# The second feed-forward of a two-layer block: 24 of its 32 token tiles sorted by expert, 8 left dense

## The reference, cut to what matters

```
logits = tanh(x @ Wg1.T) @ Wg2.T                    # x: 4096 x 256, layer-normed
_, top_idx = top_k(logits, 2)
scores[token, top_idx] = softmax(top_logits)         # zero for the other six
up   = einsum('td,ehd->teh', xt, Wup) + bup          # e: 8, h: 128
h    = silu(up)
down = einsum('teh,eoh->teo', h, Wdown) + bdown
out  = einsum('te,teo->to', scores, down)
x    = x + tanh(g_ffn[1]) * out
```

## Time and profile before

| | |
|---|---|
| time, median of 3 runs | 1808.64 us (1806.33 to 1809.66) |
| profiled execution | 1795.94 us, span 1794.1 us |
| first attention, first feed-forward | to about 830 us |
| second attention, last residual | 1520.2 us |
| last block's residual, end of the last output | 1790.6 us, 1794.1 us |

### The profile page before, as it was taken

The page is one execution under the profiler, slowest core; times in us unless marked ns, Lnnn a source line. Parts: engine busy times, 40 slices in busy tenths (PEclk is TensorE's granted clock), DMA queues, the critical chain, the costliest instruction groups (busy, mean ns, idle before and its releaser), DMA issues.

```text
span 1794.1 us, 42480 instructions
## 1 busy us (share of the span) xinstructions
PE 1619.7 (90%) x14740; PEld 1361.1 (76%) x14740; DVE 1160.6 (65%) x3029; ACT 738.2 (41%) x1508; POOL 423.3 (24%) x464
## 2 busy tenths in 40 slices
PE   3899999978998899998799999999999997799998
PEld 2566666656776689997688888888888886578887
DVE  5888888886567655456466666666666654465655
ACT  2466666652322225554333333333333332344443
POOL 3555555522224210000222111221221111000000
PEclk8999999999999999999899999999999998799999
DMA  7566666642101015433200000000000000000000
GB/s 203 114 126 126 124 125 126 125 74 67 38 30 42 24 42 156 143 124 111 77 27 22 20 26 21 20 23 27 20 26 20 21 15 6 1 24 12 12 24 24
DMA packets 127357, 107.07 MB, mean 60 GB/s; under 512 B 10442, under 2 KB 120195, under 8 KB 127020
## 3 DMA queue, kind: packets, MB, share of 16 engines
q1 hardware_dynamic: 121068, 89.07, 21.2%
q0 software_dynamic: 6208, 16.95, 2.9%
HBM read 49.22 MB, written 56.77 MB: 59 GB/s over the span
## 4 chain that ended last, share of the span: by engine, by line
PE 53%; DVE 24%; issue 10%; ACT 6%; SPq 3%; DVEq 1%; DMA 1%; ACTq 1%
PE bank L544 10%; PE bank L546 9%; PE bank L545 9%; PE bank L1020 4%; PE bank L606 3%; PE bank L615 2%; PE bank L1048 2%; PE bank L629 2%; PE bank L570 2%; DVE rm_b L2281 2%; PE bank L646 2%; DVE rs_b L2289 2%; DVE probs_b L2284 1%; DVE oT_b_lo L2273 1%; PE bank L633 1%
## 5 line engine op out<-in xcount | busy, mean ns | idle before, releaser
L544 PE MATMUL bank<-xT_b_hi,m_hi 128*128 128x256 f32 x512 | 154.1, 301 | 23.9 <-ACT qT L1390 12.0
L1411 ACT ACTIVATE probs_b<-probs_b 128x512 f32<-128x512 f32 x64 | 40.4, 632 | 324.9 <-DVE probs_b L2284 324.9
L1584 POOL TENSOR_TENSOR probs_b<-probs_b,rs_b 128x512 f32<-128x512 f32 x64 | 66.8, 1043 | 454.0 <-DVE rs_b L2294 453.7
L544 PE MATMUL bank<-n_hi,oT_b_hi 128*128 128x256 f32 x512 | 149.7, 292 | 5.8 <-DVE x L2252 5.8
L545 PE MATMUL bank<-xT_b_hi,m_lo 128*128 128x256 f32 x512 | 145.8, 285 | 0.0
L546 PE MATMUL bank<-xT_b_lo,m_hi 128*128 128x256 f32 x512 | 145.7, 285 | 0.0
L545 PE MATMUL bank<-n_hi,oT_b_lo 128*128 128x256 f32 x512 | 145.1, 283 | 0.0
L546 PE MATMUL bank<-n_lo,oT_b_hi 128*128 128x256 f32 x512 | 145.0, 283 | 0.0
L1194 ACT ACTIVATE probs_a<-probs_a 128x512 f32<-128x512 f32 x128 | 80.4, 628 | 114.4 <-DVE probs_a L1723 114.0
L1020 PEld LDWEIGHTS bank<-ctxT_b,qT 128*128 128x128 f32 x1024 | 125.2, 193 | 2.7
L544 PEld LDWEIGHTS bank<-xT_b_hi,m_hi 128*128 128x128 f32 x512 | 98.9, 193 | 30.5 <-ACT qT L1390 15.0
(11 more groups left out here) (316 smaller groups left out, 4786.7 us busy)
## 6 DMA issues: line engine op xcount, KB each, us to landing
sorted_x<-zeros SPq DMA_DIRECT2D x16, 2112.0 KB, 14.7
xg<-sorted_x SPq DMA_DIRECT2D x71, 128.0 KB, 2.1
sorted_y<-ys SPq DMA_DIRECT2D x71, 128.0 KB, 2.0
w_raw<-in_w SPq DMA_DIRECT2D x16, 408.0 KB, 3.8
x<-in_x SPq DMA_DIRECT2D x4, 1024.0 KB, 7.1
cx_raw<-in_ctx SPq DMA_DIRECT2D x32, 128.0 KB, 2.6
out<-x SPq DMA_DIRECT2D x8, 512.0 KB, 2.9
ctxT_a<-in_ctxT SPq DMA_DIRECT2D x16, 128.0 KB, 2.2
```

The costliest lines, as they stand in the source:

```text
L544: pe.matmul(dst, lh, rh, start=start, stop=False, skip_group_check=True)
L1584: pool.tensor_tensor(probs_b[b], probs_b[b], rs_b[:, b, :].unsqueeze(2).broadcast_to([P, G1, S]), ALU.mult).then_inc(s["b_probs"], 1)
```

## The change

The first 24 token tiles take the routed form in the second feed-forward; the last 8 stay dense, in two blocks.

- Routing goes into attention rounds 2 to 13 (`NR = 12`), always for the two tiles of two rounds before: TensorE gets `turn_f`, `logits_f`, `back_f` and `place_f`, ScalarE `xh_f` and `tanh_f`, VectorE `xl_f`, `largest_f`, `counts_f`, `slots_f` and at the round's end `norm_f`, GpSimd four scatters (`scatter_f`). `setup_f` is in round 1, the table of tiles (`table_f`, `places_f`) in round 14. The loop body now holds two rounds.
- The weights' halves move out of the rounds: ScalarE makes eight pieces of 512 columns in round 15, where the copies of queries were, and GpSimd the eight low pieces after its last probabilities.
- NJ1 = 31 tiles of 256 sorted rows follow the attention: loads with three buffers and two tiles ahead, two Silus for each tile on ScalarE (one full, one rounded), the bias added on VectorE in `y_x2`, and the expert's up-weights copied to a fixed place by GpSimd (`stage`). SyncE loads `bd1`, all eight output biases for all partitions (1 MB), before the third tile.
- The preparation of the first dense block stands between these tiles.
- After the last store GpSimd gathers 24 x 2 times (`gather_f`, three buffers); VectorE adds (`add_f`) nine tiles within the first dense block and fifteen within the second.
- The separate pass for mean and deviation (`stats`, with a square root on ScalarE) is gone; a reciprocal root on VectorE takes its place.

```diff
@@ SyncE @@
+            def load_rows1(j):
+                if j >= NX1:
+                    sp.wait_ge(s["x_xT_psum"], NJ + j - NX1 + 1)
+                row = sp.value_load(row1[0:1, j:j + 1], min_val=0, max_val=ROWS - R1)
+                sp.dma_start(xg1[j % NX1], xs_dram[ds(row, R1), :].rearrange("(t p) d -> p t d", p=P)).then_inc(s[f"x{j % NX1}_loaded"], 16)
+            def store_rows1(j):
+                sp.wait_ge(s["x_y_ready"], NJ + j + 1)
+                sp.dma_start(ys_dram[j * R1:(j + 1) * R1, :].rearrange("(t p) d -> p t d", p=P), ys1[j % NY1]).then_inc(
+                    s[f"x_stored{j % NY1}"], 16)
...
             sp.wait_ge(s["b_resid"], START + NA * 2)
+            sp.dma_start(bd1.rearrange("p e n -> p (e n)"), a["bdown"][0:E, :].rearrange("e n -> (e n)").unsqueeze(0).broadcast_to([P, E * D])).then_inc(s["w1_loaded"], 16)
+            sp.wait_ge(s["c_added"], NT)
+            for j in range(NJ1 + 2):
+                if j + NX1 - 1 < NJ1:
+                    load_rows1(j + NX1 - 1)
+                if j >= 2:
+                    store_rows1(j - 2)
@@ TensorE, attention round @@
-                scores1(i, 0)
+                scores1(i, 0, route is not None or late or last)
+                if route is not None:
+                    turn_f(i, route)
                 rest(outputs1, 3)
...
                 ahead(turn_x1)
+                if route is not None:
+                    logits_f(i)
                 rest(project1, 1, 1)
+                if route is not None:
+                    back_f(i)
                 ahead(queries1, 0)
                 scores1(i, 3)
                 turn_probs1(i, 0, last)
-                ahead(queries1, 1)
+                ahead(queries1, 1, route)
...
                 turn_probs1(i, 2, last)
+                if route is not None:
+                    place_f(i)
@@ TensorE, sorted tiles @@
+            for j in range(NJ1 + 2):
+                if j + 1 < NJ1:
+                    turn_x2(j + 1)
+                if j < NJ1:
+                    up_x2(j)
+                expert_f(j + 1)
+                if j >= 2:
+                    down_x2(j - 2)
+                if j == 10:
+                    turn(0, 0, 0)
+                if j == 13:
+                    turn(0, 0, 1)
+                if j == 16:
+                    pe.wait_ge(s["rw_split"], 3)
+                    logits(0, 0)
+                if j == 18:
+                    logits_back(0, 0)
+                if j == 22:
+                    turn_weights(0, 0)
...
+            for i in range(BLOCKS1):
+                block_(i, i % 2, i + 1 < BLOCKS1)
@@ ScalarE @@
+            def silu_x2(j):
+                n = NJ + j
+                e = act.value_load(exi1[0:1, j:j + 1], min_val=0, max_val=E - 1)
+                act.wait_ge(s["x_gu_psum"], n + 1)
...
+                act.activation(hs1[j % 2], bank[2 + j % 2][:, 0:R1], ACT.Silu, bias=bup[:, ds(e, 1)]).then_inc(s["x_silu"], 1)
+                act.activation(hgh1[j % NH1], bank[2 + j % 2][:, 0:R1], ACT.Silu, bias=bup[:, ds(e, 1)]).then_inc(s["x_hh_ready"], 1)
@@ GpSimd @@
+            def stage(j):
+                e = pool.value_load(exi1[0:1, j:j + 1], min_val=0, max_val=E - 1)
+                if j >= 2:
+                    pool.wait_ge(s["x_gu_psum"], NJ + j - 1)
+                for n, w in enumerate((w1_hi, w1_lo)):
+                    m = pool.tensor_copy(up1[j % 2][:, n], ffn1_view(w)[0][:, :, ds(e * P, P)])
+                m.then_inc(s["w1_split"], 1)
...
+            def gather_f(tile):
+                n = tile % NG1
+                if tile >= NG1:
+                    pool.wait_ge(s["c_added"], NT + tile - NG1 + 1)
+                done = s[("y_gathered", "y_gathered1", "y_gathered2")[n]]
+                for c in range(TOP):
+                    pool.indirect_dma_start(out=yg_f[n][:, c, :], out_offset=None, in_=ys_dram,
+                                            in_offset=bass.IndirectOffsetOnAxis(ap=place_of[:, c, tile:tile + 1], axis=0)).then_inc(done, 16)
@@ VectorE, attention round @@
                 weigh(0)
+                if route is not None:
+                    xl_f(i)
                 centre(2)
                 weigh(1)
                 if not last:
                     xT_low1(i + 1)
+                if not first and route is None and more:
+                    setup_f()
+                if route is not None:
+                    largest_f(i)
+                    counts_f(i)
                 centre(3)
...
                 if not last:
                     mask_row(i + 1)
+                if route is not None:
+                    slots_f(i)
+                if late:
+                    table_f()
                 otl(i, 2)
                 ptl(i, 3)
+                if late:
+                    places_f()
                 if more:
                     add_tile(i * 2 + 5)
                     stats_b(i + 2)
+                    if not first:
+                        norm_f(i - 1, 0 if route is None else 1 - route, None if route is None else i // 2 - 1)
@@ VectorE, sorted tiles @@
+            for j in range(NJ1 + 2):
+                if j + 1 < NJ1:
+                    xl_x2(j + 1)
+                if j < NJ1:
+                    hl_x2(j)
+                if j >= 2:
+                    y_x2(j - 2)
+                if j == 2:
+                    rsqrt(rstd[:, FIRST_DENSE:NT], nmr[:, FIRST_DENSE:NT], 8, NT - FIRST_DENSE, mv[:, FIRST_DENSE:NT, :])
+                if j == 8:
+                    norm(0, 0)
+                if j == 10:
+                    split_bias()
...
@@ VectorE, dense block @@
+                    if i == 0 and t >= 1:
+                        add_f(t - 1)
+                    if i == 1:
+                        add_f(9 + t + t // 2)
+                        if t % 2 == 1:
+                            add_f(10 + t + t // 2)
```

More of the change, by code:

```diff
@@ L701, in _ @@
             pe.sem_inc(s["a_loop_done"], 1)
[L703 to L713, removed]
-                    else:
[L715 to L723, removed]
+            ph, f, chunks, hidden = "f1", f1, NC1, HID1
@@ new lines, in _, with turn @@
+            gate, gated = None, False
+            up, down = zip(*(ffn1_view(w) for w in (w1_hi, w1_lo)))
+            last = {c: (hidden - c * P if (c + 1) * P > hidden else P) for c in range(chunks)}
+            NL = E + 1 if gated else E
+            def turn(i, u, k):
+                pe.wait_ge(s[f"{ph}_xn_ready"], START + i + 1)
+                if k == 0:
+                    pe.wait_ge(s[f"{ph}_cTl_ready"], START + i)
+                else:
+                    pe.wait_ge(s[f"{ph}_xl_ready"], START + i * KT + k)
+                for t in range(FT):
+                    m = pe.transpose(bank[6][:, t * P:(t + 1) * P], f["xn"][:, t, k * P:(k + 1) * P], ident)
+                m.then_inc(s[f"{ph}_xnT_psum"], 1)
@@ L724, in logits @@
                     for k in range(KT):
-                        m = split3(bank[6][0:NL, :], (f["rw_hi"][:, k, 0:NL], f["rw_lo"][:, k, 0:NL]),
+                        m = split3(bank[b + c % 2][0:M, :], (w[0][:, k, cols], w[1][:, k, cols]),
                                    (f["xh"][u][:, k, :], f["xl"][u][:, k, :]), k == 0, k == KT - 1)
[L727 to L739, removed]
@@ L1413, in next_q @@
                 def next_q(*cs):
-                    if not last:
+                    if last:
+                        for c in cs:
+                            w1_high(c)
+                    else:
                         for c in cs:
@@ L1952, in ffn @@
[L1952 to L1964 removed]
+                    other = f["s"][c % 2]
@@ L2278, in centre, with attend1 @@
+            def attend1(i, first=False, route=None, late=False, last=False):
+                more = not late and not last
                 def centre(b):
@@ L2338, in _ @@
             attend1(0, first=True)
-            with ve.Fori(1, NA - 2) as i:
-                st.loop(i, STEPS["b"], 1)
-                attend1(i)
-            st.end(NA - 2)
-            attend1(NA - 2, more=False)
-            attend1(NA - 1, more=False, last=True)
+            attend1(1)
+            with ve.Fori(1, NR // 2 + 1) as j:
+                st.loop(j, STEPS["b"], 1)
+                for u in range(2):
+                    attend1(j * 2 + u, route=u)
+            st.end(NR // 2 + 1)
+            attend1(NA - 2, late=True)
+            attend1(NA - 1, last=True)
             otl(NA - 1, 3)
@@ L2357, in _layouts @@
+            for i in range(BLOCKS1):
+                block_(i, i % 2, i + 1 < BLOCKS1)
+            st.wait()
 def _layouts(v):
```

959 lines of the change are left out of this document (642 added, 317 removed).

## The result

The changed kernel is slower: 1825.54 us median of 4 runs (1824.47 to 1828.03) against 1809.15 us (1806.33 to 1812.31), a ratio of 1.0092 with a 95% interval of 1.0072 to 1.0112. I had forecast 1771.6 us, a range of 1728 to 1802, and 0.11 for "slower".

A forecast was written before the change was run, and what follows sets the result against it. TensorE was busy 90% of the span, but VectorE's chain was taken to set the attention round's end. Attention +32 us and second feed-forward -69 (205 for 273.9) gave -37: 1771.6 us, range 1728 to 1802.

The forecast's parts named there:

- The step that failed: Attention routing rounds: turn_f's 0.48 us hidden by VectorE's chain; TensorE's other added work and waits 1.3 us a round.
- Rival (c): Routing rounds: hand-offs over three engines exposed, from 5.5 us a round; 8 with counts_f, giving 1839 us; chance 0.11.
- The small costs: Routing rounds: 2.4 us each, the small routing operations costed at nothing under named covers; +32 us over the attention.
- The sorted tiles: Second feed-forward, y(0) to y(30): load chain binds, 7.8 us for two tiles, between 6.8 and 8.6; 117 us.
- Rival (a): Sorted tiles: loads hidden, VectorE bounds each tile at 2.4 us, 72 in place of 117; 1727 us, chance 0.14.
- The tail: From y(30) to the end: gathers beside two dense blocks, 75 us, with one 3.5 us GpSimd stop for an add.
- The base: Whole kernel: runs' median 12.7 us above the profiled execution; that difference put onto the forecast median, 1757 becoming 1771.6.

The follow-up runs named there:

- e5: The changed kernel with both edits: turn_f behind outputs1(i-1, 3) and the second half of project1(i-1, 0), VectorE's loop written out; 1775.46 us, ratio 0.9795.
- e2: The changed kernel with only VectorE's loop over the twelve routing rounds written out as straight code; 1813.35 us, ratio 1.0019.
- e1: The changed kernel with only TensorE's turn_f moved behind outputs1(i-1, 3) and the second half of project1(i-1, 0); 1802.27 us, 0.995 of before.
- e6: As e5, with VectorE's norm_f also moved from the round's end to behind the next round's first subtraction, centre(0); 1770.3 us, ratio 0.9762.
- e13: The changed kernel with the edits of e1, e2, e6 and e3, repeated in a set without late signals; 1712.49 us, before 1795.64.
- e3: The changed kernel with SyncE storing sorted tile j-3 instead of j-2 behind the load of tile j+2; 1787.49 us, ratio 0.9873.
- e15: The changed kernel once more, unedited, in a set without late signals; 1805.28 us, before 1795.64, ratio 1.006.
- e8: The kernel before once more, unedited, for a second profile; 1814.58 us in one execution.
- e7: The changed kernel issuing 6 of the 48 gathers, other adds using rows not gathered anew; 1811.03 us.

## Why the prediction was wrong

**The step that failed** is the one on TensorE's new work: "turn_f (4 transposes, 0.48) lies in the time that VectorE's chain takes anyway". Its duration does; its wait does not. My sum has norm_f lengthening VectorE's end, and turn_f needs norm_f's result, but I did not ask what stands behind turn_f in TensorE's order: outputs1(3) and a half of project1, which were the cover of VectorE's end. They moved out from under it to behind it. By e5 against e2, with the loop written out in both, this cost 1813.4 - 1775.5 = 38 us; before took 1811 and 1812 us beside them.

**A second cost was not in the sum at all:** the jump back of VectorE's loop, whose body became two rounds with 122 counted steps in place of one with 41 (STEPS in the kernel). VectorE stands 3.1 to 3.7 us at each of five edges in every profile with the loop; before, whose loop holds one round, has no idle over 0.7 us ahead of a round's first maximum. By e5 against e1 it cost 27 us, 5.4 an edge, more than the gap itself, and TensorE's clock is lower there (0.96 in a 47-us round of e1, 1.00 in the next of 42). The two hid each other: alone they gave 23 and 12 us, together 50. The Trainium skill (Runtime: NRT & Kernel Launch, "Instruction fetch mechanics") says that a taken branch to code outside the engine's small window must fetch it first. The trace agrees, with 3.1 us or more at each edge and none without the loop. That the gap is such a fetch is not shown: the profile names nothing for it, and no run had a loop of another length. I had not looked the page up.

**Rival (c)** had the right kind of cause (hand-offs exposed, from 5.5 us a round) and largely the wrong place: not the chain of hand-offs inside the round, of which no later one adds to TensorE's waits (the other two groups of its waits in these rounds are those of before, under 1 us each), but the first of them at its edge, and with it the loop's jump, which it did not have. Measured 5.6 us a round, just its threshold, which is in part luck. Its time of 1839 us was 13 too high, as counts_f was not exposed: VectorE still stands 0.88 us ahead of the fourth maximum, waiting for TensorE.

**The small costs** were over-priced: with both waits gone the round is +1.2 us (e5), +0.9 (e6), where I had 2.4. xl_f, largest_f, counts_f, slots_f, xh_f and tanh_f lay under their covers. In e13, with the two waits gone and norm_f moved, the attention ends 11 us later than in before, not 32. The Tanh takes 0.36 us, and no table load stands beside it in the rounds.

**The sorted tiles** went as forecast: 121.7 us against 117, loads binding, clock 0.80 and so between the two levels that bounded my 7.8 us for two tiles; measured 8.1. My sum had a slip: its terms as listed add up to 7.4 us and not 7.1, and with the same half-way choice 7.8 becomes 8.1. e3 shows the chain to be the one described: one step more of slack and the stage drops by 36 us. Rival (a), 2.4 us a tile, is not reached even so, at 2.9.

**The tail** was mis-sized by 6 us (75, measured 81.3 without late signals, 86 to 87 with them). I had GpSimd stopping once for an add, 3.5 us. In e15 an add releases it nine times, 9.8 us in all, because VectorE's adds come in its program order; five of these waits are no longer than the 0.30 us that stand between any two gathers, and the other four are 4.0, 2.8, 1.0 and 0.5 us.

```profile
POOL yg_f L1885 <- DVE x L2804: 9.8, 9, 4.0
```

How much of the 6 us these stops are, no run separates.

**The base.** I put the 12.7 us between profile and median onto the median. For what both kernels share that was right, without my knowing the cause. Between the sets with and without late signals before differs by 13.5 us and the changed kernel by 20.3, so about 7 us more, and its tail, where it now gathers, is 5.5 us longer in the profile with them. That goes with a ratio of 1.009 in the one and 1.006 in the other.

## What to carry to other kernels

When an instruction with a new wait goes into an in-order queue, price what stands behind it, not the instruction: here 0.5 us of transposes cost about 3 us a round (38 us over twelve), and moving them behind work that was ready gave it back. Two waits at one place hide each other, so undo both before you call either harmless. Take two profiles of the kernel before and compare each with the median; if they differ, find the stage before you subtract stages.

## What the hardware showed that I had not expected

- VectorE with two rounds in its loop (122 counted steps) stood 3.1 to 3.7 us at each jump back, with no releaser in the profile ("issue"); with one round in it (41) it did not, and with all twelve rounds written out (e2) it did not either.
- In some sets of runs TensorE's signals reach ScalarE and VectorE late while GpSimd issues indirect DMAs back to back: 20.1 us of ScalarE's idle at 456 in e8, 7.5 and 10.5 us in the dense blocks of the changed kernel, none there with 6 gathers in place of 48. In the dense blocks both engines start within 0.03 us of each other, and in the places shown they start 1.8 and 2.6 us after the last DMA of a run. The same programs show none of it in other sets of runs, and before is then 1796 us and not 1810. That they go when most of GpSimd's gathers go is shown for the dense blocks by e7; why some sets of runs (or chips) have it, and what holds the signals, stays open.
- Slack pays twice where the clock is low: one more step between load and store took TensorE's waiting for loads from 43 to 11 us and its busy time from 79 to 67, at a granted clock of 0.81 and then 0.96.
